# One block's first scores and first vector update moved into the block ahead, and the product of level 64 in 64 columns

## The reference

```python
h = layernorm(x) * (1 + ca) + sa
q, k, v = silu(h @ wq), sigmoid(h @ wk), h @ wv          # 4 heads of 128
f = 1 - k;  theta = cumsum(sign(f - 0.5)) * PI
qr, kr = [q cos, q sin], [k cos, k sin]
S = S * exp(log f) + kr_t v_t^T;   o_t = (scale * qr_t) S  # a scan over the rows
out = layernorm(o * sigmoid(h @ wg1 @ wg2)) * norm_w @ wo
x = x + ga * out
# feed-forward: r = sigmoid(xr @ W_r), out = r * (relu(xk @ W_k)**2 @ W_v); x = x + gb * out
```

## Time and profile before

| what | us |
|---|---|
| median of 3 runs | 1828.87 |
| lowest, highest | 1828.83, 1833.27 |
| profiled execution, whole | 1829.41 |
| its span in the trace | 1827.5 |
| PE busy | 1791.9 (98%) |
| DVE busy | 1494.7 (82%) |
| ACT busy | 736.8 (40%) |
| POOL busy | 376.0 (21%) |

### The profile page before, as it was taken

How to read it: one execution, slowest core, us unless ns; L and a number is a source line. 1 busy time by engine, 2 the same in 40 slices (tenths; PEclk the granted TensorE clock), 3 DMA queues, 4 the chain that set the end, 5 groups by cost and what they waited for, 6 DMA issues and landing times.

```text
span 1827.5 us, 48846 instructions
## 1 busy us (share of the span) xinstructions
PE 1791.9 (98%) x20777; PEld 1611.8 (88%) x20777; DVE 1494.7 (82%) x3465; ACT 736.8 (40%) x1425; POOL 376.0 (21%) x309
## 2 busy tenths in 40 slices
PE   6999999999999999999999999998999999999998
PEld 5898889998999989998999989987888989889887
DVE  5988878888888888888888888899787787877875
ACT  3433433334333343333433343344445454454443
POOL 1010110100111011110101001112343434434343
PEclk9999999999999999999999999999999999999999
DMA  6011002100001000110001000020211111111110
GB/s 242 3 48 48 25 25 71 47 26 25 25 25 48 25 25 25 38 36 25 25 25 48 25 25 25 25 71 24 83 57 70 47 69 59 58 70 52 65 58 35
DMA packets 42623, 84.40 MB, mean 46 GB/s; under 512 B 2324, under 2 KB 2856, under 8 KB 42408
## 3 DMA queue, kind: packets, MB, share of 16 engines
q1 hardware_dynamic: 42392, 81.28, 12.5%
q10 hardware_dynamic: 16, 0.00, 0.0%
HBM read 47.72 MB, written 33.55 MB: 44 GB/s over the span
## 4 chain that ended last, share of the span: by engine, by line
PE 93%; DVE 4%; issue 1%; ACT 1%; DMA 0%; POOL 0%; SPq 0%; POOLq 0%; DVEq 0%; ACTq 0%
PE bank L1209 63%; PE lvl L1209 9%; PE bank L1326 3%; PE bank L1319 3%; PE bank L1217 3%; PE bank L1318 3%; PE lvl L1285 3%; PE bank L1246 2%; PE lvl L1268 1%; PE bank L1310 1%; PE lvl L1304 1%; PE lvl L1298 1%; DMA mod_raw<-in_L_wmod 0%; DVE xk L914 0%; DVE xr L914 0%
## 5 line engine op out<-in xcount | busy, mean ns | idle before, releaser
L131 POOL TENSOR_TENSOR ln_rs<-ln_ve,mhalf 128x2 f32<-128x2 f32 x64 | 82.9, 1295 | 872.5 <-DVE ln_ve L126 872.5
L1209 PE MATMUL bank<-hT_hi,wq_hi 128*128 128x256 f32 x512 | 151.4, 296 | 4.4 <-DVE wq_lo L1148 4.4
L356 POOL TENSOR_TENSOR xs<-xs,y 128x512 f32<-128x512 f32 x64 | 83.1, 1299 | 334.1 <-DVE y L731 334.1
L1209 PE MATMUL bank<-xk_hi,fk_hi 128*128 128x256 f32 x512 | 146.3, 286 | 3.8 <-DVE xk_lo L927 3.8
L1209 PE MATMUL bank<-hT_hi,wk_hi 128*128 128x256 f32 x512 | 148.9, 291 | 0.0
L1209 PE MATMUL bank<-xk_lo,fk_hi 128*128 128x256 f32 x512 | 146.0, 285 | 0.0
L1209 PE MATMUL bank<-xk_hi,fk_lo 128*128 128x256 f32 x512 | 145.9, 285 | 0.0
L1209 PE MATMUL bank<-hT_lo,wk_hi 128*128 128x256 f32 x512 | 145.7, 284 | 0.0
L1209 PE MATMUL bank<-hT_hi,wk_lo 128*128 128x256 f32 x512 | 145.4, 284 | 0.0
L1209 PE MATMUL bank<-hT_lo,wq_hi 128*128 128x256 f32 x512 | 145.4, 284 | 0.0
L1209 PE MATMUL bank<-hT_hi,wq_lo 128*128 128x256 f32 x512 | 145.2, 284 | 0.0
(11 more groups left out here) (208 smaller groups left out, 5797.0 us busy)
## 6 DMA issues: line engine op xcount, KB each, us to landing
xs<-in_L_attn_x SPq DMA_DIRECT2D x32, 512.0 KB, 3.8
x_scratch<-xs SPq DMA_DIRECT2D x32, 512.0 KB, 3.2
xs<-x_scratch SPq DMA_DIRECT2D x32, 512.0 KB, 3.6
out<-xs SPq DMA_DIRECT2D x31, 512.0 KB, 2.8
mod_raw<-in_L_wmod SPq DMA_DIRECT2D x6, 1024.0 KB, 7.9
raw_q<-in_L_attn_wq SPq DMA_DIRECT2D x1, 1024.0 KB, 5.4
raw_k<-in_L_attn_wk SPq DMA_DIRECT2D x1, 1024.0 KB, 6.5
raw_v<-in_L_attn_wv SPq DMA_DIRECT2D x1, 1024.0 KB, 6.5
```

The costliest lines, as they stand in the source:

```text
L131: pool.tensor_tensor(out=ln["rs"][:, :], in0=ln["ve"][:, :], in1=mhalf[:, :], op=ALU.pow).then_inc(ln["rstd"], 1)
L356: pool.tensor_tensor(out=dst, in0=dst, in1=y[:, ch, :], op=ALU.add).then_inc(x2_sb, 1)
L1209: last = pe.matmul(dst, lhs(a, s), rhs(b, s), start=(t == 0), stop=(t == len(terms) - 1))
```

## The change

1. TensorE: `near_scores(n + 1)` runs in block n, directly behind `level_product(n, 5)`, and that pair now stands behind g1, not ahead of it. `near_scores(0)` is called once before the loop. `pair_product(n, 0)` moves from between the halves of q to the head of the block.
2. VectorE: `first_update(n + 1)` goes between `first_totals(n + 1)` and `apply_next`, `variants(n + 1)` behind `wo_scale(n - 1, 0)`, `diagonal` and `first_merge` of n + 1 behind `h_high`. `q_odd` goes ahead of `ln_stats`, `g1_low` ahead of `level_update` 64.
3. Level 64 is done in 16 calls of 64 columns, not 32 of 32, and `merge_64` copies accordingly: still two copies of 64 partitions by 256 numbers.

```diff
                 def merge_64(n, par):
-                    src = level_bank(5, par)[:, 0:G * 32].rearrange("p (g t) -> p g t", t=32)
-                    for c in range(2):
-                        last = act.copy(A[0:64, :, 64 + 32 * c:96 + 32 * c], src[64 * c:64 * c + 64, :, :])
+                    src = level_bank(5, par)[:, 0:G * 32].rearrange("p (g t) -> p g t", t=64)
+                    for o in range(2):
+                        last = act.copy(A[0:64, o::2, 64:128], src[64 * o:64 * o + 64, :, :])
...
                 def attention_body(n):          # VectorE
-                    first_update(n, par)
-                    variants(n, par, 0)
-                    diagonal(n, par)
-                    first_merge(n, par)
+                    joint(n, 0)
                     if n > 0:
                         gated_stats(n - 1, 1)
-                    joint(n, 0)
...
+                    q_odd(n + 1, 1 - par)
                     ln_stats(dve, ln, n + 2)
+                    g1_low(n + 1)
                     level_update(n, par, 64, 5)
-                    q_odd(n + 1, 1 - par)
                     ln_var(dve, ln, n + 2)
                     first_totals(n + 1)
+                    first_update(n + 1, 1 - par)
                     apply_next(n + 2)
-                    g1_low(n + 1)
...
                     if n > 0:
                         wo_scale(n - 1, 0, bank[3])
+                    variants(n + 1, 1 - par, 0)
...
                     if n + 2 < NB:
                         h_high(n + 2)
+                    diagonal(n + 1, 1 - par)
+                    first_merge(n + 1, 1 - par)
...
                         else:                   # TensorE, level_product, idx 5
-                            for c in range(2):
-                                for b in range(2):
-                                    tile = slice(32 * (b + 2 * c), 32 * (b + 2 * c) + 32)
-                                    last = pe.matmul(dst[tile, g * 32:g * 32 + 32], k[:, g, 32 * b:32 * b + 32], q[:, g, 2 + c, :],
-                                                     start=True, stop=True)
+                            for b in range(2):
+                                tile = slice(32 * (b + 2 * (g % 2)), 32 * (b + 2 * (g % 2)) + 32)
+                                out_view = dst[tile, g // 2 * 64:g // 2 * 64 + 64].rearrange("p (c t) -> p c t", c=2)
+                                last = pe.matmul(out_view, k[:, g, 32 * b:32 * b + 32], q[:, g, 2:4, :], start=True, stop=True)
...
                 def attention_body(n):          # TensorE
-                    near_scores(n, par)
+                    pair_product(n, par, 0)
...
-                    pair_product(n, par, 0)     # between the halves of q
...
                     v_rows(1)
-                    level_product(n, par, 5)
                     pe.wait_ge(q_sb, 2 * (n + 2))
                     g1_rows()
+                    level_product(n, par, 5)
+                    near_scores(n + 1, 1 - par)
```

More of the change, by code:

```diff
@@ L1196, in _ @@
                 h_high(1)
+                first_update(0, 0)
+                variants(0, 0, 0)
+                diagonal(0, 0)
+                first_merge(0, 0)
                 for n in range(LAST):
@@ L1345, in attention_body @@
                     par = n % 2
-                    near_scores(n, par)
+                    if n == 0:
+                        pe.wait_ge(mean_copied, 1)
+                    pair_product(n, par, 0)
                     if n == 0:
@@ L1358, in attention_body @@
                     rows_of("q", 0, 2, "q")
-                    if n == 0:
-                        pe.wait_ge(mean_copied, 1)
-                    pair_product(n, par, 0)
                     wait(pe, s_mid, n)
@@ L1568, in _ @@
                     gate_rows(ch)
+                near_scores(0, 0)
                 for n in range(LAST):
```

## The result

| | median, us | lowest to highest, us |
|---|---|---|
| before, in the same comparison | 1829.03 | 1828.83 to 1833.27 |
| the change | 1844.72 | 1838.31 to 1845.30 |

The ratio is 1.0074, with a 95% interval of 1.0062 to 1.0086. The change is slower by some 14 us (11 to 16 by the interval); the medians differ by 15.7. The profiled execution of it is the fastest of the four: 1838.31, with a span of 1836.4. A second measurement of the same kernel, with the experiments, gave 1.0067 (1.0052 to 1.0082). The ratios of the experiments leave out one execution, of the kernel with level 64 alone, which took 2936.6 us at a granted clock of 0.563.

What follows compares the result with a forecast made beforehand. TensorE bounds the kernel (93% of the chain), VectorE next with 2.65 us of slack at y. -12.0 + 10.8 + 0.9 + 3.7 + 7.8 - 3.2 + 1.6 = +9.6 gives 1838.5 us from the median; range 1828 to 1848.

Steps and rivals of the forecast that it cites:

- TensorE's saving: TensorE, each block: 0.29 us from fewer steps around 32-column products, 0.11 from level 64; over 30 blocks -12.0 us.
- The island: TensorE: near directly behind level 64 and pair 2 in near's old place save steps in and out, 0.29 us a block.
- rival (d): TensorE: near behind level 64 pays its own way in, so nothing is saved there; 8.7 us more, 1847; chance 0.04.
- rival (a): Level 64: 64-column records cost 9.4 ns, 5.7 us less, or y's wait is 0.25, -4.5; 1833 to 1834; chance 0.20.
- y's chain: ScalarE and VectorE from near's start N: y ready at N + 8.05, TensorE at N + 7.73, so y is late.
- What the wait costs: TensorE at state_step: waiting for y costs 0.40 us a block (0.25 to 0.75), +10.8 us over 27 blocks.
- The second race: Block end: gated(n, 1) on VectorE against t2(n, 1) on TensorE just holds, 0.03 us a block, +0.9 us.
- Rival (b): y in time through a shorter operation or earlier ScalarE; chain 0.4 shorter, gated(n, 1) 0.2 earlier: 1824 us; chance 0.10.
- Three special blocks: Blocks 15, 16 and 30: y's wait is worse by 0.4, 0.9 and 1.2 us, +3.7 with rounding as predicted.
- Start-up: Block 0: pair 2 waits 3.2 us for variants, and the second t2 starts at 94.4 instead of 86.63: +7.8 us.
- Crossing: TensorE's 3.63 us wait for xk_lo shrinks as moved VectorE work is done earlier: -3.2 us, rest lost to ogT_hi.
- Clock: TensorE: one cold spell behind new idle gaps in block 0, a third of a known window's loss: +1.6 us (0 to 5).

Runs made afterwards that it cites:

- level 64 alone: The kernel before, with only the level 64 product in 64 columns and its merge_64 changed: 1829.25 us, ratio 0.9992 to before.
- g1_high first: The change with g1_high ahead of merge_64 on ScalarE, nothing else: 1822.17 us, ratio 0.9959 to before.
- thin additions: GpSimd's two additions of a block cut to 8 of 512 columns: 1829.21 us on the change with wo_scale ahead of first_update, 1841.39 on the change.

## Why the prediction was right, and where it was off

The predicted 1838.5 is 6 us under the median of 1844.72, inside the range. The forecast case held: slower, because of y. That the profiled execution, the fastest of four, took 1838.31 is luck: in it a later start (+0.6), a dearer wait (+1.9) and a smaller gain in the crossing (+0.8) were made up by the -2.1 at block 4 and by a clock that cost nothing in block 0. By its steps:

- **TensorE's saving, 0.40 a block.** Measured 0.41 in the kernel with g1_high first. The island: 0.20 in (613.58 - 613.38, normal 0.12) and 0.34 out (615.19 - 614.85, normal 0.23), one pair of them for both products, so rival (d) fell. The record of level 64 lasts 0.65 as foreseen, so the first half of rival (a), instructions count and not columns (0.46), fell, and the second, a wait of 0.25, with the 0.40 below.
- **y's chain.** `g1_low` was put at N + 1.4 and began at 615.48 - 614.05 = N + 1.43. y was put at N + 8.05 and ended at N + 8.06. PE would have come at 621.77 = N + 7.72, put at N + 7.73. The wait of 0.40 is there. This step took every length from rows of before, and it held to hundredths.
- **What the wait costs.** Here a term was too small. A block is 0.52 longer than with g1_high first, not 0.40. 0.10 of the difference is the product behind the wait: `state_step` takes 1.89 to the next row (624.06 - 622.17), and 1.79 without a stop (616.11 - 614.32 with g1_high first; its record is 2.05 where before has 1.95). Over 30 blocks it is 3 us, which the sum did not have. It is most of the excess in the fifth line of the table (3.1 and 2.9 for 1.2).
- **The second race, +0.9.** No wait at t2 shows in mid blocks of the change. That it would hold PE by 0.2 if y came sooner was right (37.52 against 37.33), but only where y alone comes sooner. With g1_high first `g1_low` starts at N + 0.04 instead of N + 1.43, y ends 1.39 earlier and `gated(n, 1)` 0.50 earlier (N + 16.05 instead of 16.55, as VectorE now waits for PE in between), and both races are won. "A wait of about 0.25 is a floor" was therefore wrong as a general statement: it took for granted that only y would move. Rival (b) asked for just this, the chain 0.4 shorter and `gated` 0.2 earlier, and named ScalarE as one way. Nothing in the change itself does it.
- **Three special blocks, +3.7.** Block 16 is right (0.97 over before, 0.87 over a normal block's 0.10), and block 30 is some 2.0 late (1.87 printed as idle), put at 1.6. Block 15 has the extra wait of 0.4 that was foreseen: `state_step` starts 0.81 late (660.01 - 658.98 less 0.22). But its step is 0.10 like the others, since in before PE waits for `g1_lo` in just this block, its one wait of the earlier trace rows, and in the change it does not: from the keys to `output` it takes 2.27 there and 1.82 here. This gain of 0.4 is what the sum left out. The change, then before:

```profile
658.98 0.39 PE L1317 MATMUL bank<-V,A 128*128 128x128 f32 x2
660.01 1.16 PE L1324 MATMUL bank<-V,Kt 128*128 128x128 f32 x8 [0.65 <-DVE y L731]
```
```profile
649.16 0.50 PE L1209 MATMUL bank<-wg_hi,g_hi 128*128 128x512 f32 x1 [0.19 <-DVE g_lo L715]
```

- **Start-up, +7.8.** `t2` of block 1 went from 86.63 to 95.04, and near of block 0 began 0.63 later in that trace: 7.8. The three waits on the way are those named (3.20, 3.12, 1.56), with one for the keys (1.26) that was not counted by itself.
- **Crossing, -3.2.** With block 30's wait for y the step was put at -2.0 and came out at -1.2 and -0.2, with a wait for xk_lo of 4.49. The mechanism is there, and 1 to 2 us less of it: the wait of pair 2 for `variants` (2.1 us in before) is gone and that for ogT_lo fell from 3.0 to 1.4, but xk_lo's grew by 0.9. A new wait for ogT_hi, to which the prediction put the rest, does not show.
- **Clock, +1.6 (0 to 5).** As far as two traces tell, what the median is off lies mostly here and in the start. The granted clock over the span was 0.998 in the profiled execution and 0.992 to 0.994 in the other three, which took 6 to 7 us longer. The second trace shows some of the places (windows of the first profile, then of the second; the third number from the end is the granted clock):

```profile
40.00:110.00 70.00, 60.86 (x1054) 52.79 (x1053) 58.26 (x158) 25.46 (x49) 1.75 (x2) 1.00 0.01 2
...
1250.00:1270.00 20.00, 17.35 (x156) 15.52 (x156) 18.97 (x38) 11.26 (x22) 6.01 (x5) 0.85 0.15 53
```
```profile
40.00:110.00 70.00, 62.34 (x1043) 54.61 (x1042) 57.62 (x153) 24.46 (x47) 1.75 (x2) 0.95 0.01 2
56.00:58.00 2.00, 2.00 (x12) 2.00 (x10) 2.00 (x4) 0.00 (x0) 0.00 (x0) 0.50 0.00 0
90.00:100.00 10.00, 6.80 (x98) 6.07 (x98) 9.78 (x22) 2.69 (x6) 0.00 (x0) 0.83 0.01 2
```

Behind the wait of 3.20 in block 0 the clock is at its lower level (1.2 GHz) for a while in the second and not in the first, and again between 90 and 100, where PE waited 3.11 us for the state. The second trace loses 1.5 more in this stretch (8.9 against 7.4). The two spells take some 3.4 us of full clock (0.05 x 70), and the wait of 1.56 ahead of t2 is not there, as PE comes later. It loses 1.0 more in the crossing, 0.6 at block 4, where both have a clock of 1.00 and only the stop is longer, and 1.9 ahead of near of block 0. That start moves between 47.6 and 50.4 us over the traces of this study, with before's at 47.85, and was not in the sum at all. So of the 4.7 between the two traces 2.5 lie where the clock falls, and 2 in the start. The executions of 1844 to 1845 us left no trace. One spell at a third of a known one was too little for such a run; and since only one trace of before was read, how often its own runs start late stays open.

## What to carry to other kernels

When a step moves ahead on one engine, write down the whole chain from its release to the next reader with a start for each operation. Look first at what stands ahead of the releasing operation on a third, lightly loaded engine: here swapping two operations on ScalarE, busy 40%, turned 12 us more than before into 7.6 less. A step that is moved away may be the cover of a wait elsewhere (near covered `gated` at t2), and one that is moved ahead also releases its other readers sooner (y started GpSimd's addition beside VectorE's work). At the two ends of a pipeline the old order may be the better one, and it can be kept for the first blocks alone.

## What the runs showed of the hardware

- A VectorE operation with two SBUF inputs that started within GpSimd's 128x512 addition took 1.76 instead of 0.68 (128x512) and 1.09 instead of 0.39 (128x128), and the addition 1.65 instead of 1.28 when VectorE had begun first. In one order of the kernel thin additions took 39 us off 1868, 32 of them by the length of a block. In another order (the change) it was the addition that took 2.06, and VectorE lost nothing beside it.
- A matmul group of 16 records behind a wait of 0.4 took 0.10 longer than without one (1.89 to the next row for 1.79), and the same 1.89 behind the waits of block 16 (1.12 printed) and block 30 (1.87).
- Behind a gap of 3.2 us on TensorE at the same place of the same program the granted clock stayed at 1.00 in one execution, and in another it was 0.50 over 56 to 58 us.
- Products on 32-column tiles: 32 records of 64 columns last 0.65, 64 of 48 columns 0.86 to 0.89, 64 of 32 columns 0.76. Two such products behind one another cost one step in (0.08) and one out (0.11).
